# A two-layer graph network kernel: z rows written by indirect scatters from GpSimd instead of DMAs from SyncE

## What is computed

```python
# layer 1
aggr = segment_sum(edge_attr_64, src)
x = x + relu(concat[h, aggr] @ W1 + b1) @ W2 + b2      # h = relu(layernorm(x))
# layer 2, h = relu(layernorm(x)) of the new x
z = h @ W_fc.T
z_src = z[src]; z_dst = z[dst]; ex = e @ W_edge.T
a = z_src @ blk[0] + z_dst @ blk[K] + ex @ w_e
for k in range(1, K):                                  # moments of z_src and z_dst over all edges
    a = a + src_m[k] @ blk[k] + dst_m[k] @ blk[K + k]
att = where(a > 0, a, SLOPE * a)
w = softmax of att over the edges of one dst
out = x + segment_sum(w[:, None] * (z_src + ex @ W_e2n.T), dst)
```

## Time and profile before

| | us |
|---|---|
| median of two runs | 5636.81 |
| span of the profiled execution, first to last instruction | 5658.6 |
| POOL busy in it | 4128.6 |
| DVE busy in it | 2664.5 |
| PE busy in it | 2057.3 |
| ACT busy in it | 806.1 |
| first gather of z rows (L521) | 3397.8 |
| last gather of z rows | 5499.1 |

### The profile page before, as it was taken

How to read it: one execution, slowest core, us unless ns; L and a number is a source line. 1 busy time by engine, 2 the same in 40 slices (tenths; PEclk the granted TensorE clock), 3 DMA queues, 4 the chain that set the end, 5 groups by cost and what they waited for, 6 DMA issues and landing times.

```text
span 5658.6 us, 56864 instructions
## 1 busy us (share of the span) xinstructions
PE 2057.3 (36%) x12714; PEld 1848.6 (33%) x12715; DVE 2664.5 (47%) x7488; ACT 806.1 (14%) x2465; POOL 4128.6 (73%) x3165
## 2 busy tenths in 40 slices
PE   0244444444444444444444375332333233233330
PEld 0233333333333333333333254222222222222220
DVE  1333333333333333333333476666666666666661
ACT  0000000000000000000000132222222222222220
POOL 0388888888888888888888507777777777777760
PEclk9999999999999999999999966555555555555555
DMA  2544444444444444444444462222222222222211
GB/s 80 186 37 35 35 37 35 35 37 35 35 37 35 35 37 35 35 35 36 35 35 37 103 119 29 34 34 33 33 33 33 33 33 33 34 33 33 33 30 47
DMA packets 609215, 245.64 MB, mean 43 GB/s; under 512 B 563804, under 2 KB 578268, under 8 KB 605537
## 3 DMA queue, kind: packets, MB, share of 16 engines
q0 software_dynamic: 275968, 104.57, 23.5%
q1 hardware_dynamic: 330251, 132.61, 10.2%
q10 hardware_dynamic: 2902, 7.58, 0.4%
HBM read 151.66 MB, written 92.65 MB: 43 GB/s over the span
## 4 chain that ended last, share of the span: by engine, by line
POOL 61%; issue 21%; DMA 6%; SPq 3%; PE 3%; DVE 1%; POOLq 1%; ACT 0%; ACTq 0%; DVEq 0%
POOL acc_dram L495 35%; POOL zg L521 27%; DMA acc_dram<-y_sb,idx 5%; SPq L355 2%; SPq L349 1%; PE bank L841 1%; PE bank L776 1%; DMA acc_dram<-work 1%; PE bank L768 0%; PE bank L761 0%; SPq L337 0%; POOLq L493 0%; PE bank L769 0%; ACT work L637 0%; PE bank L808 0%
## 5 line engine op out<-in xcount | busy, mean ns | idle before, releaser
L495 POOL DMA_INDIRECT acc_dram<-y_sb,idx x1568 | 2496.5, 1592 | 686.7 <-issue 434.1
L521 POOL DMA_INDIRECT zg<-z_dram,idx x1568 | 1624.7, 1036 | 667.5 <-issue 667.2
L751 PE MATMUL bank<-ea_sb,same 128*128 128x66 f32 x3136 | 771.0, 427 | 1746.9 <-DVE same L999 1746.9
L751 PEld LDWEIGHTS bank<-ea_sb,same 128*128 128x128 f32 x3136 | 698.2, 328 | 1829.5 <-DVE same L999 1233.4
L1010 DVE SCALAR_TENSOR_TENSOR todummy<-y_sb,threshold,todummy 128x4 f32<-128x4 f32 x392 | 87.2, 223 | 1835.2 <-ACT y_sb L561 1835.2
L637 ACT ACTIVATE work<-work,f_s 128x80 f32<-128x80 f32 x1568 | 416.2, 347 | 997.8 <-DVE work L1217 997.8
L561 ACT ACTIVATE y_sb<-bank 128x264 f32<-128x264 f32 x392 | 153.3, 391 | 2833.9 <-POOLq L493 2778.2
L852 PE MATMUL bank<-ident,f_top 128*80 128x128 f32 x196 | 85.0, 434 | 1201.4 <-DVE f_top L1250 1201.4
L860 PE MATMUL bank<-zg,work 128*80 128x68 f32 x3136 | 455.0, 340 | 2.2 <-ACT work L647 2.2
L860 PEld LDWEIGHTS bank<-zg,work 128*80 128x80 f32 x3136 | 441.8, 253 | 2.4 <-ACT work L647 2.4
L852 PEld LDWEIGHTS bank<-ident,f_top 128*80 128x80 f32 x196 | 27.6, 141 | 1239.4 <-DVE f_top L1250 1239.4
(11 more groups left out here) (218 smaller groups left out, 2818.7 us busy)
## 6 DMA issues: line engine op xcount, KB each, us to landing
ea_sb<-in_edge_attr_dram SPq DMA_DIRECT2D x195, 256.0 KB, 3.3
acc_dram<-work SPq DMA_DIRECT2D x24, 1072.5 KB, 18.2
work<-acc_dram SPq DMA_DIRECT2D x112, 227.5 KB, 3.9
acc_dram<-y_sb,idx POOLq DMA_INDIRECT x1568, 3.2
zg<-z_dram,idx POOLq DMA_INDIRECT x1568
f_t<-t_dram SPq DMA_DIRECT2D x196, 40.0 KB, 2.9
tab<-tab_dram SPq DMA_DIRECT2D x196, 20.9 KB
tab_dram<-tab SPq DMA_DIRECT2D x196, 20.9 KB, 1.5
```

The costliest lines, as they stand in the source:

```text
L495: g_.indirect_dma_start(out=acc_dram[g][:, :], out_offset=bass.IndirectOffsetOnAxis(ap=idx[:, s, g:g + 1], axis=0), in_=y_sb[:, s, g * EW: ...
L521: g_.indirect_dma_start(out=zg[:, s, g, 0:ZW], out_offset=None, in_=z_dram[:, :], in_offset=bass.IndirectOffsetOnAxis(ap=idx[:, s, g:g + 1 ...
L751: ins = t_.matmul(banks[4 + h][:, j * EW:(j + 1) * EW], same[:, h, j, :], ea_sb[:, s, 4 * h + j, :], start=True, stop=True)
```

## The change

The seven DMAs L390 and their waits for s_z go from SP. In their place POOL, after the memsets of zg and before its wait for s_zst, waits for s_z to reach c + 1 and issues 14 indirect DMAs for chunk c: each writes column b of z_sb, one row of 65 floats per partition, to row p * 98 + b of z_dram for every partition p. There is no compute_op, so each is a plain write. The row numbers come from z_rows, a new tile of 128 x 98 integers that one iota fills at the program's start. The wait for s_zst now asks for 16 * 98.

```diff
+        z_rows = sb("z_rows", [P, NB], I32)
...
-            for c in range(NB // CZ):
-                sp.wait_ge(s_z, c + 1)
-                sp.dma_start(z_dram.rearrange("(p b) c -> p b c", p=P)[:, c * CZ:(c + 1) * CZ, :],
-                             z_sb[:, c * CZ:(c + 1) * CZ, 0:ZW]).then_inc(s_zst, 16)
...
+            chain(g_.iota(z_rows[:, :], pattern=[[1, NB]], base=0, channel_multiplier=NB))
...
-            pool.wait_ge(s_zst, 16 * (NB // CZ))
+            for c in range(NB // CZ):
+                pool.wait_ge(s_z, c + 1)
+                for b in range(c * CZ, (c + 1) * CZ):
+                    g_.indirect_dma_start(
+                        out=z_dram[:, :], out_offset=bass.IndirectOffsetOnAxis(ap=z_rows[:, b:b + 1], axis=0),
+                        in_=z_sb[:, b, 0:ZW], in_offset=None).then_inc(s_zst, 16)
+            pool.wait_ge(s_zst, 16 * NB)
```

## The result

The changed kernel takes 5729.16 us (median of 5728.94 and 5729.39), before 5636.81: ratio 1.0161, 95% interval 1.0142 to 1.0181, 92.4 us slower. The forecast was 5728.

The account below looks back on a forecast made before the run. POOL was taken to set the pace from first to last gather. First gather 103.6 us later, less 12 us given back, made +91.6 us on 5636.8: forecast 5728 us, range 5714 to 5790.

Parts of the forecast that it names:

- POOL sets the pace and the late start arrives at the end: Attention gathers: each microsecond the first gather starts later is a microsecond at the end, unless later gathers run quicker.
- Only the first chunk is waited for: POOL's scatters of z: scatters start at 3355.7 us; the other six chunk waits cost nothing.
- The scatter at the gather's price: Each plain scatter on POOL: 0.945 + 0.305 = 1.25 us, so 97 steps are 121.2 us.
- Rival 1: POOL's scatters: a plain one costs what an adding one does, 58.0 us more, 5786 us; chance 0.28.
- Stalls beside DVE, 21 us: Scatters held on POOL by DVE instructions: 10.5 us at four long ones, 8.4 at the first four, 2 at small ones.
- three cases: Scatters beside the first four long DVE instructions: one slips through each, 8.4 us (taken); none, up to 13.4; spared, less.
- Landing, 3.5 us from the last scatter's start to the first gather: POOL's wait after the last scatter: 3.3 us to land in DRAM plus 0.2 to restart.
- Rival 2: Scatters don't overlap, each costs its landing: 323 us instead of 146, 5905 us; chance 0.03, shared with other losses.
- First gather 103.6 us later: Start of the attention gathers on POOL: at 3501.4 us instead of 3397.8.
- The gathers give back 12 us: First to last gather: 10.5 us of stalls no longer fall there, another count gives 15 us; 12 taken.
- Rival 3: Attention loop: a later start shifts gathers against DVE's work, up to 131 us back, not slower from 92; chance 0.03.
- one sign of being wrong that I had named: Last gather on POOL: the forecast is wrong if it isn't later than before by some 90 us.

Follow-up runs that it names:

- double_2: The changed kernel with every column of z scattered twice, the second time into a copy nobody reads (196 scatters): 5858.0 us.
- adding_2: The changed kernel with its 98 scatters adding into a z_dram that SP filled with zeros at the start: 5789.1 us, ratio 1.0257.
- one_input: The changed kernel with DVE's four third-power multiplications (two SBUF inputs) replaced by sums over one input, so other output: median 6148.9 us, ratio 1.0241.
- psum_means: The changed kernel with the means of DVE's four subtractions read from PSUM instead of SBUF: 5722.4 us, ratio 1.0140.
- again_after: The changed kernel, unchanged, run and profiled again on another chip: 5733.4 us, ratio 1.0159.
- before_3: The kernel before, unchanged, run and profiled again on another chip: run 5643.8 us, profile span 5642.0 us.

## Why the prediction came out

Point by point:

- **POOL sets the pace and the late start arrives at the end.** Right, and shown: 124.6 us for 98 more scatters, with the gather phase unchanged (double_2).
- **Only the first chunk is waited for.** Nearly. The first scatter came 150.7 us behind the start of the memsets in after, where SP's first DMA had come 149.1 us behind them in before. All other waits for z are counted with 0.3 us, the step that every DMA of POOL's has.
- **The scatter at the gather's price.** Right: 0.962 us measured, 0.945 taken. 97 steps at 1.265 instead of 1.25 are 1.5 us more. Rival 1 is excluded by that row, and adding_2 shows the price it would have had, +56.0 us; the rival said 58.
- **Stalls beside DVE, 21 us.** Measured 142.7 - 97 x 1.265 = 20.0. The first four cost 8.4 as taken, the others 10.0, the small ones of L1113 1.5. one_input and psum_means show the cause as named. That one scatter slips through at each of the first four, which I chose among three cases, came out too. The Trainium skill, "SBUF — State Buffer", section "Who interferes with whom", says that a DVE instruction with two SBUF inputs contends with a GpSimd instruction that reads SBUF; the traces of after and again_after agree, with scatters of 3.0 to 3.9 us beside two SBUF inputs, and so do one_input and psum_means, with 0.96 beside a reduction or an input in PSUM. The statement in the same list that tensor_tensor was not seen to stall DMAs of GpSimd doesn't hold for these indirect ones.
- **Landing, 3.5 us from the last scatter's start to the first gather.** Measured 3.2. Landing itself is 2.2 us; the restart takes 1.0, not 0.2. Two errors that cancel: I had taken the adding scatter's landing, and the addition lengthens that too. Rival 2 (serial landings) is excluded: scatters start 1.27 us apart and land 2.2 after issue.
- **First gather 103.6 us later.** Measured 105.3 and 108.1, of which 1.1 and 4.0 are node work ahead of the first scatter. From the first scatter to the first gather I had 145.7 us; it took 146.0 and 145.9.
- **The gathers give back 12 us.** Measured 15.5 and 18.1 against before_3. Of these, 10.5 were the long DVE instructions that now meet scatters. The rest of the 18.1 in again_after is an early stretch that I had set at nothing: from the 49th to the 151st gather before_3 needs 209.9 - 71.1 = 138.8 us and again_after 192.8 - 60.8 = 132.0 (starts counted from the first gather of each). That is 1.361 and 1.294 us for each gather, where both kernels later come to 1.33. In before this is where DVE catches up with POOL, a block each 8.1 us instead of 10.65, so that more of its instructions fall on each gather; after the change DVE begins right behind POOL and has nothing to catch up. This can account for about half of the 6.8 us, what lies above the later rate. The other half is that the first gathers of the changed kernel run faster than its later ones, at about 10.2 us for a block while DVE works on the 14 blocks that stand ahead of its loop; why is open. Neither was tested by a run.
- **Sum.** Predicted +91.6, measured +92.4 and +89.8; in the profiles +89.8 and +90.0 against before_3. The measured ratio leaves 80 to 102 us, and the terms were off by up to 4.5 us (first gather) and 6.1 us (gathers) in opposite directions, so that the sum came within 2 us is luck in part; that the loss is the row of scatters with its stalls and one landing, less some 15 us, is not. Rival 3 (a late start shifts the phase of the loop) had no part: from 3700 to 5400 us before_3 makes 1280 gathers and after 1279.

The one thing that I read wrongly is a reference: I put the first profile's difference to its runs, 21.8 us, evenly on both kernels. It belonged to that one execution. The difference of the two kernels came from durations and steps, so it didn't suffer. But one sign of being wrong that I had named did: the last gather was to be later by some 90 us, and against the first profile it is later by 67.9 only (5567.0 and 5499.1). Against before_3 it is later by 84.7, and by 89.2 in again_after.

## What to carry to other kernels

A step that its own engine can't start before the others are done costs its full length when that engine is the one that sets the pace afterwards, even if it stood idle for 190 us before, as here (double_2: 98 more scatters, 124.6 us). An idle stretch on the engine is worth something only if the inputs of the new work are there at its start. A ring of buffers bounds what an earlier start can gain: before speeding up the producer, look at when its first buffer is given back.

## What the runs showed of the hardware that I had not expected

- A z DMA of SP with 260-byte pieces keeps the 16 DMA engines full for 45 us (the view adds up to 104.6% of their time); the same rows written by POOL's scatters need 8.7% (1536 packets in 60 us, 48 scatters). Per row that is 45 us x 1.046 x 16 / 12544 = 60 ns of one engine, against 60 us x 0.087 x 16 / (48 x 128) = 14 ns. The scatters go out as 32 packets for 128 rows, SP's DMAs as one packet per row.
- The kernel before took 6002 us on one chip and 5637 to 5644 on the others, and that chip's traces show PE at one matmul per 2.80 us while plain scatters ran, and not while adding ones did. The cause is open. Whoever compares a time with one from another chip can read a 6% loss into an unchanged kernel.
